# Graph layer with routed experts on one core: token counters as a table, and three small GpSimd jobs of the middle stage handed to a transfer and to ScalarE

## The chip, the cores and the metric

The kernel runs on one core of a Trainium2 chip. A core has a matrix engine (TensorE, PE in the profile, with its weight loads shown apart as PEld), a vector engine (VectorE, DVE), a scalar engine (ScalarE, ACT), a general engine (GpSimd, POOL) and a queue engine (SyncE, SP) that here only issues transfers. Engines run on their own and meet at semaphores: an instruction waits until a counter has reached a value, and a finished instruction raises a counter. The metric is the device time of one execution in microseconds (us). Three runs of the kernel before took 1539.47, 1539.72 and 1540.53 us, so the median is 1539.72 us. A change within 0.2% (3.1 us) is not told from no change.

## The reference, cut to what matters

There are 12,500 tokens of 256 numbers, and an edge list of which only the first 12,500 entries of `src` and `dst` matter here.

```python
xn = layernorm(x)
# graph part: heads 4 x 64; softmax over the heads
xt = (xn @ W).reshape(-1, 4, 64)
alpha = softmax(leaky_relu(alpha_l[src] + alpha_r[dst], 0.01), axis=1)
tmp = einsum('nh,nhd->nd', alpha[:n], xt[dst[:n]])     # a row of a table, gathered by dst
# linear attention with 8 heads, elu + 1, over all tokens
x = x + broadcast(tmp over heads) + mix(xn)
# routed experts: 8 experts, each token goes to the one with the largest logit
logits = layernorm(x) @ gate_w + gate_b
idx, prb = argmax(softmax(logits)), its probability
pos = how many earlier tokens chose the same expert     # kept while pos < capacity
y = (relu(rows @ w1[e] + b1[e]) @ w2[e] + b2[e]) * prb
x = x + nan_to_num(y)
```

## The kernel before, in words

The 12,500 tokens are worked on as 25 tiles of 500 (`NS = 25`, `TS = 500`): 125 partitions (`T`) with 4 tokens each (`J`). There are three stages, each a block in which every engine has an instruction list of its own.

**First stage** (L146 to L625, to 367 us). Layer norm, queries and keys, and per token a row of `graph_table` (values, scores and gate logits of each of 4 heads) and of `alpha_l_table`, both written to memory in HBM. What the gate logits owe to the token itself stays on chip in `xl_all`, and the edge indices are read into `idx_all` (both hold all 25 tiles). GpSimd sets constants here, among them the counters `tokn` and `ntokn` (L325, L327).

**Middle stage** (L628 to L1227, 367 to about 762 us), the one that the change touches. Each engine walks the 25 tiles with `over_steps` (L735): tiles 0 and 1 written out, tiles 2 to 21 in a hardware loop of two tiles per turn, tiles 22 to 24 written out. Buffers with two halves are picked by `par`, the parity of the tile. In step `s`:

- SyncE (`step`, L771) waits until the output of tile `s` is in `xd`, stores it, waits for the matrix products of tile `s` and loads the input of tile `s + 2` into `x_sb`. In step 22 it then starts the loads of the first expert's weights (`first_expert`, L749).
- GpSimd (`step`, L821) waits for the first product `pr` of tile `s` (the gathered rows of the same parity have then been read), issues the eight indirect transfers that gather the rows of tile `s + 2` (`gather`, L792: four into `gl`, four into `gx`, L797), copies the indices of tile `s + 3` out of `idx_all` (`idx_of`, L786, once the gathers that read that half of `idx` have landed), copies the logits of tile `s + 2` into the last columns of `x_sb` (`xl_of`, L801) and steps the two token counters by 500 (`token_of`, L806: `tokn` holds token number plus one, `ntokn` its negative). It does so after ScalarE has used the counters of tile `s - 1` (`s_at_ready`).
- ScalarE (`step`, L905): the square root of the variance (`root`), the transposed inverse (`inverse_t`), a copy of the queries (`q_copy`), two exponentials (`logit_exp`, `att_exp`), and `one_hots` (L869). That last one turns the place given to each token into a row and a column one-hot: `nprb`, eight `Abs` activations into `away`, then, after waits for its own results and for `s_token`, twelve `Relu` activations. In four of these the counters are the bias and the scale (L890). Square root and exponential are in different activation tables, so every step has two table loads.
- VectorE (`step`, L1055): `rows_of` (sum `xd`, statistics), `den_of`, `logits` (its first instruction, L1009, needs the root), `choose`, `att_scores` and `q_scaled` of tile `s + 1`, `place` (writes `prb`, `block_f`, `row_f`), `att_sum` of tile `s + 1` (the three large `pr` instructions).
- TensorE (`step`, L1205): `x_part(s + 1)` (needs `x_sb` with its logits, `s_xl`), `inverse`, `listed(s - 1)` (the one-hots, L1200), `den_spread`, `positions`, `mix(s + 1)` (L1175) and `q_ksum(s + 2)`.

Ahead of its steps GpSimd copies two sets of indices, gathers tiles 0 and 1, copies the indices of tile 2 and then the logits of tiles 0 and 1 (L812 to L819).

**Third stage** (L1229 on, to the end). The eight experts on the rows listed in the middle stage. The change does not touch it.

Of the kernel before, what the change touches and what calls it, by code (L numbers as in the profile page):

```python
# [56 lines left out]
def gps_layer(nc, x, src, dst, gnn_w, attn_l, attn_r, wq, wkv, wproj, bproj,  # L57
# [49 lines left out]
    with base:  # L107
        def sb(name, shape, dt=F32):
            return sb_in(base, name, shape, dt)
# [14 lines left out]
        tokn = sb("tokn", [T, J])  # L124
        ntokn = sb("ntokn", [T, J])
# [20 lines left out]
        with ExitStack() as ph, nc.Block() as block:  # L146
# [134 lines left out]
            def _(pool):  # L281
# [43 lines left out]
                nc.gpsimd.iota(tokn[:, :], [[1, J]], base=1 - TS, channel_multiplier=J,  # L325
                               allow_small_or_imprecise_dtypes=True)
                nc.gpsimd.iota(ntokn[:, :], [[-1, J]], base=TS - 1, channel_multiplier=-J,  # L327
# [300 lines left out]
        with ExitStack() as ph, nc.Block() as block:  # L628
# [61 lines left out]
            s_idx = sem_in(ph, "s_idx")  # L690
# [35 lines left out]
            s_token = sem_in(ph, "s_token")  # L726
# [5 lines left out]
            x_in, gat, x_out = [s_x_in0, s_x_in1], [s_gat0, s_gat1], [s_x_out0, s_x_out1]  # L732
            NATT, NPR, NLG, NROUTE, NPLACE, NAWAY = 7, 3, 3, 11, 4, 9
# [14 lines left out]
            def _(sp):  # L748
# [18 lines left out]

                load(0, 0)
                load(1, 1)

                def step(s, par, h, ahead):  # L771
                    sp.wait_ge(s_x2_ready, 2 * (s + 1))
                    split_dma(sp, tok(out, s, D), xd[:, par, :, :], T, x_out[par])
                    if ahead == 2:
                        sp.wait_ge(s_mix_mm, 2 * (s + 1))
                        load(s + 2, par)
                    if ahead == 2 and isinstance(s, int) and s == NS - 3:
                        first_expert()
# [6 lines left out]
            def _(pool):  # L785
                def idx_of(s, par, n):  # L786

                    pool.wait_ge(gat[par], 32 * J * n)
                    nc.gpsimd.tensor_copy(idx[:, par, :, :], idx_all[:, bass.ds(s, 1), :, :].rearrange("p a n j -> p (a n) j"))\
                      .then_inc(s_idx, 1)  # L790

                def gather(s, par):  # L792
                    pool.wait_ge(s_idx, s + 1)
                    passed(pool, s_pool_passed)
                    for n, (to, of) in enumerate(((gl, table_l), (gx, table))):
                        for j in range(J):
                            pool.indirect_dma_start(out=to[:, par, j, :], out_offset=None, in_=of,  # L797
                                                    in_offset=bass.IndirectOffsetOnAxis(ap=idx[:, par, n, j:j + 1], axis=0))\
                                .then_inc(gat[par], 16)

                def xl_of(s, par):  # L801
                    pool.wait_ge(s_mix_mm, 2 * (s - 1))
                    nc.gpsimd.tensor_copy(x_sb[0:T, par, :, D:MW],
                                          xl_all[:, bass.ds(s, 1), :, :].rearrange("p a j e -> p (a j) e")).then_inc(s_xl, 1)

                def token_of(s):  # L806
                    pool.wait_ge(s_at_ready, 3 * J * s)
                    passed(pool, s_pool_passed)
                    nc.gpsimd.tensor_scalar(tokn[:, :], tokn[:, :], float(TS), None, ALU.add).then_inc(s_token, 1)
                    nc.gpsimd.tensor_scalar(ntokn[:, :], ntokn[:, :], float(TS), None, ALU.subtract).then_inc(s_token, 1)  # L810

                idx_of(0, 0, 0)  # L812
                idx_of(1, 1, 0)
                gather(0, 0)
                gather(1, 1)
                idx_of(2, 0, 1)
# [4 lines left out]
                def step(s, par, h, ahead):  # L821
                    if ahead == 2:
                        pool.wait_ge(s_pr, NPR * s + 1)
                        gather(s + 2, par)
                        if not (isinstance(s, int) and s + 3 >= NS):
                            idx_of(s + 3, 1 - par, h + par + 1)
                        xl_of(s + 2, par)
                    token_of(s)
# [6 lines left out]
            def _(act):  # L835
# [16 lines left out]
                for c in range(KC):  # L852
                    act.wait_ge(s_mixw_mm, KC)
                    act.activation(mix_w[:, c, :], psM[:, KC + c, 0:MW], ACT.Copy).then_inc(s_mixw_set, 1)

# [13 lines left out]
                def one_hots(s):  # L869
# [14 lines left out]
                    act.wait_ge(s_token, 2 * (s + 1))  # L884
                    passed(act, s_act_passed)
                    for j in range(J):
                        act.activation(at_row[:, j, :], away[:, j, 0:T3], ACT.Relu, bias=1.0, scale=-1.0)\
                           .then_inc(s_at_ready, 1)
                        for n, (v, nv) in enumerate(((tokn, ntokn), (prb, nprb))):
                            act.activation(at_block[:, j, n, :], away[:, j, T3:T3 + NB], ACT.Relu, bias=v[:, j:j + 1],  # L890
                                           scale=nv[:, j:j + 1]).then_inc(s_at_ready, 1)
# [13 lines left out]
                def step(s, par, h, ahead):  # L905
# [6 lines left out]
                    if ahead > 0:  # L912
                        att_exp(s + 1)
                        one_hots(s)
                    else:
                        last_rows(s)
# [5 lines left out]
            def _(dve):  # L922
# [160 lines left out]
                dve.wait_ge(s_token, 2 * NS)  # L1083
                dve.wait_ge(s_perm_mm, NS - 1)
                for j in range(J):
                    for n, v in enumerate((tokn, prb)):
                        nc.vector.tensor_scalar(at_block[:, j, n, :], upto[:, T3:T3 + NB], blk[:, j:j + 1], v[:, j:j + 1],
# [627 lines left out]
```

## Time and profile before

| | before |
|---|---|
| median of three runs | 1539.72 us |
| the profiled execution | 1540.95 us |
| its span, first to last instruction | 1539.1 us |
| mean granted TensorE clock, share of full | 0.943 |
| busy PE, DVE, ACT, POOL | 1426.4, 1122.5, 952.0, 727.3 us |
| middle stage, about | 367 to 762 us |

The profile gives each engine's busy time, then the span in 40 slices, then the groups of instructions by cost, and the trace behind it can be asked for one stretch, one line or all waits. "Busy" says how much an engine did, not whether the end depended on it: for that the waits are read. A wait "A <- B" means that A's engine sat idle and that B's end is what let it go on; "issue" stands for time in which nothing that the profile shows was waited for. In rows of a timeline the first number is the start, the second the length, and the bracket at the end is the idle time just before. A line number is that of the kernel before.

### The profile page before, as it was taken

Reading aid. Unit: us, or ns where it says so; the run is one execution under the profiler, and the core shown is the slowest. Engines: PE = TensorE matmul, PEld = TensorE weight load, DVE = VectorE, ACT = ScalarE, POOL = GpSimd, SP = SyncE. Lnnn points to the kernel's source line nnn. Section 1 sums busy time; section 2 is a strip of 40 time slices with the busy share of each in tenths; the row PEclk is TensorE's granted clock in tenths of the full one; section 3 lists DMA queues with packets and bytes.
Section 4 is the critical chain, followed back from the end, with each engine's and each line's share of the span. In section 5 each row is a group of like instructions: output and inputs, shape, how many; then the busy total and the mean of one; then the engine's idle time right before and its main releaser. Section 6 shows DMA issues by size and latency. Waiting matters only on the chain. (4 is left out here: it accounts for less than half of the span.)

```text
span 1539.1 us, 30428 instructions
## 1 busy us (share of the span) xinstructions
PE 1426.4 (93%) x9008; PEld 1282.6 (83%) x9008; DVE 1122.5 (73%) x2832; ACT 952.0 (62%) x2017; POOL 727.3 (47%) x704
## 2 busy tenths in 40 slices
PE   5999999998799898899579999999999999999995
PEld 4999999997677777777469999999999999999994
DVE  5888888883678778778536867767776776877764
ACT  2555555542477777777556767667676676767662
POOL 1100000003788888888243446445446445455533
PEclk8999999997788988988779999999999999999998
DMA  4434333333344444445312121213113131122000
GB/s 85 87 80 80 86 83 74 86 73 74 93 111 109 117 109 111 116 109 157 73 31 78 31 57 44 71 39 97 43 40 91 40 95 43 39 69 53 7 15 19
DMA packets 128116, 112.13 MB, mean 73 GB/s; under 512 B 66078, under 2 KB 113887, under 8 KB 127946
## 3 DMA queue, kind: packets, MB, share of 16 engines
q1 hardware_dynamic: 75206, 72.73, 19.0%
q0 software_dynamic: 52864, 38.82, 11.5%
q8 instruction: 24, 0.39, 0.1%
q14 instruction: 22, 0.18, 0.0%
HBM read 76.17 MB, written 43.85 MB: 78 GB/s over the span
## 5 line engine op out<-in xcount | busy, mean ns | idle before, releaser
L1390 POOL DMA_INDIRECT out<-q_all,to_i x128 | 176.3, 1378 | 328.6 <-issue 293.8
L1592 DVE TENSOR_TENSOR h_lo<-q_all,h_hi 128x496 fp32r<-128x496 f32 x256 | 173.8, 679 | 197.7 <-PE psY L1653 88.4
L1468 ACT ACTIVATE h_hi<-psH,b_sb 128x496 fp32r<-128x496 f32 x256 | 172.6, 674 | 232.7 <-PE psH L1676 225.7
L1653 PE MATMUL psY<-w_hi,h_hi 128*124 128x256 f32 x1024 | 289.2, 282 | 0.0
L1653 PE MATMUL psY<-w_hi,h_lo 128*124 128x256 f32 x1024 | 287.1, 280 | 0.0
L1653 PE MATMUL psY<-w_lo,h_hi 128*124 128x256 f32 x1024 | 286.8, 280 | 0.0
L1653 PEld LDWEIGHTS psY<-w_lo,h_hi 128*124 128x124 f32 x1024 | 188.9, 184 | 8.9
L1653 PEld LDWEIGHTS psY<-w_hi,h_hi 128*124 128x124 f32 x1024 | 188.8, 184 | 8.0
L1377 POOL DMA_INDIRECT q_all<-out,from_i x112 | 164.5, 1469 | 54.8 <-issue 54.8
L1653 PEld LDWEIGHTS psY<-w_hi,h_lo 128*124 128x124 f32 x1024 | 189.1, 185 | 0.0
L1470 ACT ACTIVATE q_all<-psH,b_sb 128x496 f32<-128x496 f32 x256 | 170.8, 667 | 0.0
L1676 PE MATMUL psH<-xt_hi,w_hi 128*128 128x496 f32 x512 | 158.4, 391 | 2.4 <-issue 2.1
L1175 PE MATMUL psM<-mix_w,qp 128*125 128x264 f32 x400 | 135.1, 509 | 25.1 <-DVE qp L952 25.1
L1676 PE MATMUL psH<-xt_hi,w_lo 128*128 128x496 f32 x512 | 157.4, 389 | 0.0
L1676 PE MATMUL psH<-xt_lo,w_hi 128*128 128x496 f32 x512 | 156.6, 387 | 0.0
L292 POOL TENSOR_SCALAR rstd<-mv 125x4 f32<-125x4 f32 x25 | 5.7, 229 | 297.0 <-DVE mv L410 297.0
L1175 PEld LDWEIGHTS psM<-mix_w,qp 128*125 128x125 f32 x400 | 100.5, 257 | 52.2 <-DVE qp L952 27.4
L797 POOL DMA_INDIRECT gl<-alpha_l_table,idx x100 | 123.2, 1232 | 34.1 <-issue 29.2
L797 POOL DMA_INDIRECT gx<-graph_table,idx x100 | 121.7, 1217 | 30.5 <-issue 30.2
L1676 PEld LDWEIGHTS psH<-xt_hi,w_lo 128*128 128x128 f32 x512 | 96.6, 189 | 19.4
L1676 PEld LDWEIGHTS psH<-xt_lo,w_hi 128*128 128x128 f32 x512 | 96.6, 189 | 19.2
L371 ACT ACTIVATE eq<-psR 128x500 f32<-128x500 f32 x50 | 29.5, 589 | 89.7 <-PE psR L585 89.7
(241 smaller groups left out, 3366.6 us busy)
## 6 DMA issues: line engine op xcount, KB each, us to landing
x_sb<-in_x SPq DMA_DIRECT2D x50, 448.0 KB
q_all<-in_L_ffn_w SPq DMA_DIRECT2D x16, 1024.0 KB
graph_table<-tab_sb SPq DMA_DIRECT2D x25, 511.0 KB
out<-xd SPq DMA_DIRECT2D x25, 448.0 KB
x_sb<-in_x SPq DMA_DIRECT2D x50, 52.0 KB
out<-q_all,to_i POOLq DMA_INDIRECT x128, 4.3
q_all<-out,from_i POOLq DMA_INDIRECT x112, 4.5
gl<-alpha_l_table,idx POOLq DMA_INDIRECT x100
```

The costliest lines, as they stand in the source:

```text
L292: nc.gpsimd.tensor_scalar(rstd[:, :], mv[:, :, 1], EPS, None, ALU.add).then_inc(s_var_ready, 1)
L371: act.activation(eq[:, c, :], psR[c][:, 0:TS], ACT.Exp).then_inc(s_eq_exp, 1)
L797: pool.indirect_dma_start(out=to[:, par, j, :], out_offset=None, in_=of, in_offset=bass.IndirectOffsetOnAxis(ap=idx[:, par, n, j:j + 1], a ...
L1175: ins = nc.tensor.matmul(psM[0:T, j, 0:MW], qp[:, kc, j * T:(j + 1) * T], mix_w[:, kc, :], start=False, stop=kc == KC - 1)
L1377: pool.indirect_dma_start(out=xr[:, slot, j, :], out_offset=None, in_=out, in_offset=bass.IndirectOffsetOnAxis(ap=at[:, j:j + 1], axis=0), ...
L1390: pool.indirect_dma_start(out=out, in_=o_sb[:, par, j, :], in_offset=None, out_offset=bass.IndirectOffsetOnAxis(ap=to_i[:, par, j:j + 1], ...
L1468: act.activation(h_hi[:, f % 4, :], psH[f % 2][:, 0:TS3], ACT.Relu, bias=b1_sb[:, bass.ds(e * NF + f, 1)]).then_inc(s_hhi_ready, 1)
L1470: act.activation(hf[:, f % 4, :], psH[f % 2][:, 0:TS3], ACT.Relu, bias=b1_sb[:, bass.ds(e * NF + f, 1)]).then_inc(s_hf_ready, 1)
L1592: nc.vector.tensor_tensor(h_lo[:, f % 4, :], hf[:, f % 4, :], h_hi[:, f % 4, :].bitcast(F32), ALU.subtract).then_inc(s_hlo_ready, 1)
L1653: ins = nc.tensor.matmul(psY[par][j // 2][0:T3, (j % 2) * D:(j % 2 + 1) * D], hh[:, f % 4, j * T3:(j + 1) * T3], w[:, f, :], start=f == 0 ...
L1676: ins = nc.tensor.matmul(psH[f % 2][:, 0:TS3], w[:, kc, f * P:(f + 1) * P], xt[:, par, kc, :], start=n == 0, stop=n == 3 * KC - 1)
```

## The change

The two counters become tables `tok_all` and `ntok_all` with a column for each of the 100 (tile, j) pairs, set once in the first stage; `token_of` and the semaphore `s_token` are gone, and with them the wait in `one_hots` and the one before the last tile's columns. ScalarE reads the tables at an address that depends on the loop counter. `idx_of` moves to SyncE as a transfer from `idx_all` to `idx`, behind the load of tile `s + 2`, with a semaphore for each half. `xl_of` moves to ScalarE between `att_exp(s + 1)` and `one_hots(s)`.

```diff
-                nc.gpsimd.iota(tokn[:, :], [[1, J]], base=1 - TS, channel_multiplier=J,
+                nc.gpsimd.iota(tok_all[:, :], [[TS, NS], [1, J]], base=1, channel_multiplier=J,
                                allow_small_or_imprecise_dtypes=True)
-                nc.gpsimd.iota(ntokn[:, :], [[-1, J]], base=TS - 1, channel_multiplier=-J,
+                nc.gpsimd.iota(ntok_all[:, :], [[-TS, NS], [-1, J]], base=-1, channel_multiplier=-J,
...
             def _(sp):
+                def idx_of(s, par, n):
+                    sp.wait_ge(gat[par], 32 * J * n)
+                    sp.dma_start(idx[:, par, :, :], idx_all[:, bass.ds(s, 1), :, :].rearrange("p a n j -> p (a n) j"))\
+                      .then_inc(idx_in[par], 16)
+
+                for s in range(2):
+                    sp.dma_start(idx[:, s, :, :], idx_all[:, s, :, :]).then_inc(idx_in[s], 16)
                 load(0, 0)
                 load(1, 1)
+                idx_of(2, 0, 1)
...
                         load(s + 2, par)
+                        if not (isinstance(s, int) and s + 3 >= NS):
+                            idx_of(s + 3, 1 - par, h + par + 1)
...
             def _(pool):
-                def idx_of(s, par, n):
-                    pool.wait_ge(gat[par], 32 * J * n)
-                    nc.gpsimd.tensor_copy(idx[:, par, :, :], idx_all[:, bass.ds(s, 1), :, :].rearrange("p a n j -> p (a n) j"))\
-                      .then_inc(s_idx, 1)
-                def gather(s, par):
-                    pool.wait_ge(s_idx, s + 1)
+                def gather(s, par, n):
+                    pool.wait_ge(idx_in[par], 16 * n)
...
-                def xl_of(s, par):
-                    pool.wait_ge(s_mix_mm, 2 * (s - 1))
-                    nc.gpsimd.tensor_copy(x_sb[0:T, par, :, D:MW],
-                                          xl_all[:, bass.ds(s, 1), :, :].rearrange("p a j e -> p (a j) e")).then_inc(s_xl, 1)
-                def token_of(s):
-                    pool.wait_ge(s_at_ready, 3 * J * s)
-                    passed(pool, s_pool_passed)
-                    nc.gpsimd.tensor_scalar(tokn[:, :], tokn[:, :], float(TS), None, ALU.add).then_inc(s_token, 1)
-                    nc.gpsimd.tensor_scalar(ntokn[:, :], ntokn[:, :], float(TS), None, ALU.subtract).then_inc(s_token, 1)
-                idx_of(0, 0, 0)
-                idx_of(1, 1, 0)
-                gather(0, 0)
-                gather(1, 1)
-                idx_of(2, 0, 1)
+                gather(0, 0, 1)
+                gather(1, 1, 1)
...
                     if ahead == 2:
                         pool.wait_ge(s_pr, NPR * s + 1)
-                        gather(s + 2, par)
-                        if not (isinstance(s, int) and s + 3 >= NS):
-                            idx_of(s + 3, 1 - par, h + par + 1)
-                        xl_of(s + 2, par)
-                    token_of(s)
+                        gather(s + 2, par, h + 2)
...
             def _(act):
+                def xl_of(s, par):
+                    act.wait_ge(s_mix_mm, 2 * (s - 1))
+                    act.activation(x_sb[0:T, par, :, D:MW],
+                                   xl_all[:, bass.ds(s, 1), :, :].rearrange("p a j e -> p (a j) e"), ACT.Copy)\
+                       .then_inc(s_xl, 1)
...
                     act.wait_ge(s_away, NAWAY * (s + 1))
-                    act.wait_ge(s_token, 2 * (s + 1))
...
-                        for n, (v, nv) in enumerate(((tokn, ntokn), (prb, nprb))):
-                            act.activation(at_block[:, j, n, :], away[:, j, T3:T3 + NB], ACT.Relu, bias=v[:, j:j + 1],
-                                           scale=nv[:, j:j + 1]).then_inc(s_at_ready, 1)
+                        act.activation(at_block[:, j, 0, :], away[:, j, T3:T3 + NB], ACT.Relu,
+                                       bias=tok_all[:, bass.ds(s * J + j, 1)], scale=ntok_all[:, bass.ds(s * J + j, 1)])\
+                           .then_inc(s_at_ready, 1)
+                        act.activation(at_block[:, j, 1, :], away[:, j, T3:T3 + NB], ACT.Relu, bias=prb[:, j:j + 1],
+                                       scale=nprb[:, j:j + 1]).then_inc(s_at_ready, 1)
...
                     if ahead > 0:
                         att_exp(s + 1)
+                    if ahead > 1:
+                        xl_of(s + 2, par)
+                    if ahead > 0:
                         one_hots(s)
```

## Rows read from the trace of the kernel before

**Rows 1.** Windows: us, busy PE, PEld, DVE, ACT, POOL, then granted clock, DMA share, GB/s.

```profile
400.00:750.00 350.00, 317.78 (x1687) 264.34 (x1686) 275.02 (x1041) 259.79 (x671) 273.48 (x275) 0.87 0.47 118
```

**Rows 2.** Waits, 366 to 760 us: total us, times, longest.

```profile
ACT nprb L875 <- DVE row_f L1052: 59.2, 24, 2.9
DVE rstdb L1009 <- ACT std L863: 29.2, 23, 1.8
DVE xd L993 <- PE psM L1175: 25.4, 17, 10.6
ACT at_row L887 <- POOL ntokn L810: 16.9, 22, 0.9
DVE att L957 <- DMA gx<-graph_table,idx: 1.7, 1, 1.7
```

**Rows 3.** Timeline of one loop step, 540 to 555 us.

```profile
540.08 0.92 POOL L789 COPY idx<-idx_all 125x8 int32 x1
...
542.45 0.31 ACT L887 ACTIVATE at_row<-away 125x124 f32<-125x124 f32 x1 [0.83 <-POOL ntokn L810]
...
546.44 1.28 ACT L863 ACT_TABLE_LOAD   x1
...
548.06 0.18 DVE L1009 RECIPROCAL rstdb<-std 125x4 f32<-125x4 f32 x1 [1.67 <-ACT std L863]
...
553.54 0.21 ACT L875 ACTIVATE nprb<-prb 125x4 f32<-125x4 f32 x1 [2.44 <-DVE row_f L1052]
...
554.46 0.92 POOL L789 COPY idx<-idx_all 125x8 int32 x1
```

**Rows 4.** The page's groups: count, busy, mean ns, idle before.

```profile
L797 POOL DMA_INDIRECT gx<-graph_table,idx x100 | 121.7, 1217 | 30.5 <-issue 30.2
```

**Rows 5.** Timeline of step 0, before the waits for the counters begin.

```profile
409.26 0.21 ACT L875 ACTIVATE nprb<-prb 125x4 f32<-125x4 f32 x1 [1.65 <-DVE row_f L1052]
...
415.92 1.28 ACT L863 ACT_TABLE_LOAD   x1
...
417.54 0.18 DVE L1009 RECIPROCAL rstdb<-std 125x4 f32<-125x4 f32 x1 [0.82 <-issue]
```

**Rows 6.** Timeline: a long mix and a short one, and the roots behind.

```profile
552.31 6.64 PE L1175 MATMUL psM<-mix_w,qp 128*125 128x264 f32 x16 [1.33 <-DVE qp L952]
...
562.45 0.18 DVE L1009 RECIPROCAL rstdb<-std 125x4 f32<-125x4 f32 x1 [0.32 <-ACT std L863]
...
567.18 3.83 PE L1175 MATMUL psM<-mix_w,qp 128*125 128x264 f32 x16 [0.47 <-DVE qp L952]
...
577.35 0.18 DVE L1009 RECIPROCAL rstdb<-std 125x4 f32<-125x4 f32 x1 [1.83 <-ACT std L863]
...
736.34 0.18 DVE L1009 RECIPROCAL rstdb<-std 125x4 f32<-125x4 f32 x1 [0.32 <-ACT std L863]
```

**Rows 7.** Timeline of the start of the middle stage, GpSimd, SyncE and TensorE.

```profile
367.08 0.64 SPq L42 DMA_DIRECT2D x_sb<-in_x  x1
...
368.45 1.48 POOL L797 DMA_INDIRECT gl<-alpha_l_table,idx  x1 [1.01 <-issue]
...
386.89 1.85 POOL L797 DMA_INDIRECT gx<-graph_table,idx  x1 [0.30 <-issue]
...
393.42 0.35 POOL L819 COPY x_sb<-xl_all 125x32 f32<-125x32 f32 x2
...
393.73 3.85 PE L1168 MATMUL psM<-x_sb,ident_x 126*125 126x264 f32 x8 [7.32 <-issue]
```

**Rows 8.** DMA issues: size, then median us from issue to landing.

```profile
q_all<-in_L_mix_Wq SPq DMA_DIRECT2D x1, 256.0 KB, 4.1
```

**Rows 9.** Loop operands on ScalarE's queue (L847): min, median, max ns.

```profile
L847 ACTq FUSED_REGOPS  x20: 51/51/57, 430.9 to 706.9; - x20
```

**Rows 10.** SyncE's last load of a step, and a DMA window behind it.

```profile
546.14 0.88 SPq L43 DMA_DIRECT2D x_sb<-in_x  x1
...
549.00:551.00 2.00, 1.98 (x21) 1.80 (x19) 1.62 (x12) 1.73 (x4) 1.70 (x2) 1.00 0.42 72
```

More of the change, by code:

```diff
@@ L123, in gps_layer @@
         desc = sb("desc", [T, J, E])
-        tokn = sb("tokn", [T, J])
-        ntokn = sb("ntokn", [T, J])
+        tok_all = sb("tok_all", [T, NS * J])
+        ntok_all = sb("ntok_all", [T, NS * J])
         upto = sb("upto", [T, T3 + NB])
@@ L689, in gps_layer @@
             s_x_in1 = sem_in(ph, "s_x_in1")
-            s_idx = sem_in(ph, "s_idx")
+            s_idx0 = sem_in(ph, "s_idx0")
+            s_idx1 = sem_in(ph, "s_idx1")
             s_gat0 = sem_in(ph, "s_gat0")
@@ L725, in gps_layer @@
             s_pos_mm = sem_in(ph, "s_pos_mm")
-            s_token = sem_in(ph, "s_token")
             s_place = sem_in(ph, "s_place")
@@ L732, in gps_layer @@
             x_in, gat, x_out = [s_x_in0, s_x_in1], [s_gat0, s_gat1], [s_x_out0, s_x_out1]
+            idx_in = [s_idx0, s_idx1]
             NATT, NPR, NLG, NROUTE, NPLACE, NAWAY = 7, 3, 3, 11, 4, 9
@@ L1082, in _ @@
                 dve.wait_ge(s_place, NPLACE * NS)
-                dve.wait_ge(s_token, 2 * NS)
                 dve.wait_ge(s_perm_mm, NS - 1)
                 for j in range(J):
-                    for n, v in enumerate((tokn, prb)):
-                        nc.vector.tensor_scalar(at_block[:, j, n, :], upto[:, T3:T3 + NB], blk[:, j:j + 1], v[:, j:j + 1],
+                    for n, v in enumerate((tok_all[:, (NS - 1) * J + j:(NS - 1) * J + j + 1], prb[:, j:j + 1])):
+                        nc.vector.tensor_scalar(at_block[:, j, n, :], upto[:, T3:T3 + NB], blk[:, j:j + 1], v,
                                                 ALU.is_equal, ALU.mult).then_inc(s_at_ready, 1)
```

## The prediction, as it was put on record

> **What bounds the kernel now.** I read three views: windows of the middle stage, its waits, and a timeline of single steps. In the windows no engine of the middle stage is full: PE 317.8, DVE 275.0, ACT 259.8, POOL 273.5 of 350 us, and TensorE's granted clock is 0.87 [rows 1]. POOL's busy time hides that it is nonetheless the pace: its transfers of 1.217 us follow each other with 0.305 us of issue between (30.5 us over 100) [rows 4], so eight gathers are 8 x 1.52 = 12.2 us, and from one copy of indices to the next it is 554.46 - 540.08 = 14.38 us [rows 3]. The rest, 2.2 us, is the two copies and the two counter steps. The list of waits has none of GpSimd among the large ones; others wait for it: ScalarE 22 times, 16.9 us, before `at_row` (L887), each time for `ntokn` [rows 2].
>
> What follows a late L887 is a ring between ScalarE and VectorE. L887 late, so the table load for the root late, so the root late, and VectorE has already been standing 1.67 us at L1009 for it [rows 3]; in all 23 such waits, 29.2 us [rows 2]. From L1009 VectorE works to `row_f`, which starts ScalarE's next `nprb`. So the wait for the counters is on the path, and in most steps nothing else would catch it.
>
> **The ring without the wait, from rows.** L1009 to `nprb`: 553.54 - 548.06 = 5.48 us [rows 3]. `nprb` to the table load, in a step in which the counters were ready: 415.92 - 409.26 = 6.66 us [rows 5]. Table load to L1009: 548.06 - 546.44 = 1.62 us [rows 3], and 417.54 - 415.92 = 1.62 us in step 0 too [rows 5]. Sum 13.76 us against GpSimd's 14.38: 0.62 us less a step. The mean wait is 16.9/22 = 0.77; the other 0.15 is ScalarE's own turn-round at that point and stays.
>
> **The change part by part.**
>
> *The wait for the counters goes.* 22 steps x 0.62 = 13.6 us off ScalarE's part. What is late next is VectorE's own work: its wait at L1009 shrinks from 1.67 to 1.05 us, so in an ordinary step the whole 0.62 passes. It doesn't where the matrix product was long. With a `mix` of 6.64 us VectorE stood only 0.32 us at L1009 [rows 6], so there only some 0.3 passes. I counted six such waits of 0.32 to 0.34 us (first 446.44, last 736.34 [rows 6]). 16 x 0.62 + 6 x 0.3 = 11.7 us.
>
> *TensorE's clock.* A `mix` takes 3.83 us at 2.4 GHz and 6.64 us when it falls nearly whole into a stretch at 1.2 GHz [rows 6]; before each of them TensorE had been idle for `qp` or on very small products. A long one costs its own step and the one behind it: that next step was 577.35 - 562.45 = 14.90 us [rows 6], 0.52 above 14.38. Steps of another length move where the slow stretches fall. With none of the long ones up to 6 x (0.32 + 0.5) = 4.9 us more come off, with as many as now nothing. I can't work out the pattern; that it repeats now every four steps says only that this step length locks to it. I take two of six avoided: 1.6 us.
>
> *The start is on the path, and gets longer.* TensorE sits 7.32 us until GpSimd has copied the logits of tile 0 at 393.42, behind 16 gathers that began at 368.45 [rows 7]. They now can't begin until a transfer of indices has landed, which SyncE issues at 367.08, where now its first load is [rows 7]. Lower bound: 0.64 us of issue [rows 7] and nothing else, 367.7, where the old gather began at 368.45: 0, or 0.1 less for the copy of tile 2's indices that is gone. Upper: 4.1 us, which 256 KB took to land [rows 8], and then the 1.01 us that the first gather stood [rows 7]: 372.2, 3.7 us late. The transfer is 4 KB in 125 pieces; I take a landing after 3 us and 0.3 of issue, 370.4: 1.9 us, less the copy's 0.1 = +1.8 us. The Trainium skill ("DMA: Bandwidth & Descriptors", section "Anatomy of one DMA") gives a fixed cost of about 2.0 us to a transfer of any size; by that the start would be some 0.8 us later and the sum 1 us lower. No row here shows a small transfer by itself.
>
> *Indices in the loop.* SyncE issues them behind the load that starts at 546.14 and takes 0.88 to issue [rows 10], at about 547.0; the wait for the older gathers ahead of it is long over, since they were all issued by 540.08. Only the next step's stores queue behind it, some 12 us later. GpSimd wants them at the end of the next `pr`, over 7.5 us later (that product is running when GpSimd stands at its copy at 554.46 [rows 3]). The DMA share is down to 0.42 by 549 to 551 [rows 10]. Cost 0; with the 4.1 us of [rows 8] still 0. If it did land late, gathers have most of a step in hand: of all steps one waited for them, 1.7 us [rows 2].
>
> *GpSimd.* 12.2 us of work in 13.76. A gather beside VectorE's large products was once stretched from 1.2 to 1.85 us [rows 7]; two of them a step give 13.5, still under 13.76. The Trainium skill ("SBUF — State Buffer", section "SBUF: two separate sides") makes the port pair that VectorE and GpSimd share an exclusive lock for the length of an instruction. The 0.92 us copy, which did 8 numbers a partition beside a running `pr`, agrees with it; the rule speaks against this change in that the gathers now start just where the second and third `pr` instructions run, but even a stretch in every step leaves the sum as it is.
>
> *ScalarE's new copy.* 32 numbers a partition, about as `lex` or `nprb`, 0.2 us, in the 2.44 us in which ScalarE waits for `row_f` [rows 3]. Cost 0. Without that cover it would be 0.2 x 23 = 5 us.
>
> *Addresses from the loop counter.* Eight operands a step in 20 loop steps; one such computation is 0.051 us on ScalarE's queue [rows 9]. Bounds: 0 if the queue does them while the engine works, 8 x 0.051 x 20 = 8.2 us if each stands on the path. The activations are 0.3 to 0.5 us each and nothing waits between the twelve, so I take 0. The wider constants in the first stage fall where GpSimd is idle: 0.
>
> *Tail.* The one wait for gathers (1.7 us) is in step 23, under the expert loads. The gathers start a little earlier, the steps are shorter: 0, give or take 1. The third stage is not touched: 0.
>
> **Sum.** -11.7 - 1.6 + 1.8 = -11.5 us on the profiled execution's 1540.95 (span 1539.1 and 1.85 around it): 1529.4. The median of the runs is 1.2 us below that execution, so 1528.2.
>
> **Rivals.**
>
> 1. *The slow clock takes over (slower).* If every `mix` fell into a slow stretch, a step would be L1009 to `mix` 567.18 - 562.45 = 4.73, `mix` 6.64, and from its end (558.95) to an L1009 no longer held by the table load, 562.45 - 0.3, 3.2 us: 14.57 us. Now the mean over 22 steps is (736.34 - 417.54)/22 = 14.49. That gives 22 x 0.08 = +1.8, with the start +3.6: 1543.3. It decides from about 18 of 22 long ones: the 16.1 us of 22 x (14.49 - 13.76), less the start's 1.8, over 0.8 each. For it: shorter steps come at the clock in another phase, and one in four is long now. Against: a long one lengthens the step and so moves out of its phase.
> 2. *Addresses on the path.* 8.2 us of the gain gone: 1536.4, just inside faster. For it: the sequencer may not run ahead past the wait on `away`. Against: only the first of the twelve stands right behind a wait.
> 3. *The gap is not the counters'.* If L887 waits for ScalarE's own `away`, the profile has named the wrong one, nothing is saved and the start remains: 1541.5. Against: step 0, with the same instructions and the counters ready, took the 6.66 [rows 5].
> 4. *Indices late.* If the small transfers sit behind the loads for more than the 7.5 us and then most of a step, gathers hold `att_scores`: from there each us late costs up to 23; one us gives 1551. Against: the DMA row above.
>
> **Chances.** Forecast 0.80, rival 1 0.05, rival 2 0.09, rival 3 0.03, rival 4 0.03. About 0.2% (3.1 us) is what a measurement here tells from no change. Faster takes the forecast and most of rival 2: 0.87; same 0.06; slower 0.07 (rivals 1 and 4, part of 3). Range: at the low end no long `mix` and an instant start, 1539.7 - 13.6 - 3 = 1523, less 1 of the tail, 1522; at the high end rival 2 nearly whole, 1536.
>
> **What would show it.** Right: no wait L887 <- POOL; steps of about 13.8 us from L1009 to L1009; L1009 waiting about 1 us; GpSimd waiting for `pr` in each step; the first gather near 370.4 and the first xl copy near 395.2; the third stage as long as before. Wrong: gaps between the twelve activations (rival 2), `mix` of 6.64 us in most steps (1), GpSimd waiting for a transfer or `att` waiting for `gx` (4).

## The result and the profile after

The changed kernel takes 1527.08 us (median of 4 runs, 1525.46 to 1527.51), the kernel before 1540.12 us beside it (1539.47 to 1540.58). The ratio is 0.9914, 95% interval 0.9897 to 0.9931. The forecast was 1528.2.

(In one series, of two kernels below, the times were longer, the kernel before at 1582.88 us as well; those two kernels were run once more, beside a kernel before at 1540.18.)

The profiled execution took 1525.46 us, its span is 1523.6. I cut both spans at the same instructions: the first memset of the middle block on VectorE, and the reciprocal `rstdb` (L1009 before, L1007 after) of each step.

| stretch | before | after | difference |
|---|---|---|---|
| first stage, to the block's first memset | 367.2 | 365.1 | -2.1 |
| memset to `rstdb` of step 0 | 37.1 | 39.0 | +1.9 |
| step 0 to 1 | 13.2 | 13.2 | -0.1 |
| steps 1 to 23, 22 steps | 318.8 | 304.1 | -14.7 |
| step 23 to 24 | 15.0 | 15.7 | +0.7 |
| all behind it | 787.8 | 786.6 | -1.2 |

The first and the last line belong to code that the change doesn't touch. The first stage ended between 365.0 and 366.4 us in the experiments of the normal series, whichever kernel ran, so about 2 us of the profiled difference are its variation. The medians differ by 13.0 and the spans by 15.5: the profiled execution before was 0.8 us above its median, the one after 1.6 below.

The window of the middle stage after; columns as in [rows 1]:

```profile
400.00:750.00 350.00, 322.52 (x1708) 267.87 (x1706) 281.01 (x1078) 269.45 (x712) 225.77 (x182) 0.87 0.47 119
```

GpSimd is busy 47.7 us less than in [rows 1], though the stretch holds slightly more of the stage (1708 matmuls to 1687). ScalarE is busy 9.7 us more. The clock and the DMA share are the same.

The waits from 366 to 760 us after, to be laid beside [rows 2] (total us, times, longest):

```profile
ACT nprb L869 <- DVE row_f L1050: 55.3, 24, 2.8
...
POOL gl L803 <- DVE pr L980: 36.7, 20, 3.3
...
DVE rstdb L1007 <- ACT std L857: 18.0, 22, 1.1
```

The wait of `at_row` for `ntokn` is gone, and `rstdb` waits 18.0 us where it waited 29.2. GpSimd now has a large wait of its own: it stands for `pr` in nearly each step.

One loop step after, timeline from 540 to 555 us, beside [rows 3]:

```profile
540.94 0.77 SPq L772 DMA_DIRECT2D idx<-idx_all  x1
541.01 0.18 DVE L1007 RECIPROCAL rstdb<-std 125x4 f32<-125x4 f32 x1 [0.93 <-ACT std L857]
...
544.03 0.22 ACT L846 ACTIVATE x_sb<-xl_all 125x32 f32 x1
...
546.50 0.21 ACT L869 ACTIVATE nprb<-prb 125x4 f32<-125x4 f32 x1 [2.26 <-DVE row_f L1050]
...
549.16 0.31 ACT L880 ACTIVATE at_row<-away 125x124 f32<-125x124 f32 x1
549.26 1.40 POOL L803 DMA_INDIRECT gl<-alpha_l_table,idx  x1 [1.76 <-DVE pr L980]
...
553.15 1.28 ACT L857 ACT_TABLE_LOAD   x1
...
554.77 0.18 DVE L1007 RECIPROCAL rstdb<-std 125x4 f32<-125x4 f32 x1 [0.94 <-ACT std L857]
```

This is the ring (the chain of waits that closes on itself once a step), as forecast: L1007 to `nprb` 546.50 - 541.01 = 5.49, `nprb` to table load 553.15 - 546.50 = 6.65, table load to L1007 1.62; together 13.76. `at_row` follows its `away` without a gap.

The start, timeline, beside [rows 7]:

```profile
364.94 1.57 SPq L776 DMA_DIRECT2D idx<-idx_all  x2
...
365.06 0.17 DVE L921 MEMSET heads<- 128x128 f32 x1 [3.26 <-PEq L146]
...
368.03 1.49 POOL L803 DMA_INDIRECT gl<-alpha_l_table,idx  x1 [29.20 <-issue]
...
392.24 0.37 POOL L811 COPY x_sb<-xl_all 125x32 f32<-125x32 f32 x2
...
392.57 3.85 PE L1165 MATMUL psM<-x_sb,ident_x 126*125 126x264 f32 x8 [8.30 <-issue]
```

The first gather starts 368.03 - 365.06 = 2.97 us behind the memset, before it was 368.45 - 367.2 = 1.25: 1.7 us later. The copies of logits are only 1.0 us later (392.24 - 365.06 = 27.18, before 393.42 - 367.2 = 26.22), because a gather that took 1.85 us before [rows 7] took 1.21 here. The other 0.9 us are the first `mix`: 4.72 us at a granted clock of 0.79, where it took 3.85 at 0.97.

### The profile page after: what moved, and what is told of

Its sections match the earlier page's. It is cut to its first block and busy times, and to the rows that moved or that the text cites. A ratio compares the mean times of both kernels' runs of the same rounds, so it can differ in the third digit from the quotient of the medians.

```text
span 1523.6 us, 30383 instructions
## 1 busy us (share of the span) xinstructions
PE 1424.1 (93%) x9008; PEld 1281.1 (84%) x9008; DVE 1120.9 (74%) x2832; ACT 954.2 (63%) x2040; POOL 675.9 (44%) x606
## 5 line engine op out<-in xcount | busy, mean ns | idle before, releaser
L1172 PE MATMUL psM<-mix_w,qp 128*125 128x264 f32 x400 | 136.4, 514 | 15.5 <-DVE qp L950 15.5
L371 ACT ACTIVATE eq<-psR 128x500 f32<-128x500 f32 x50 | 29.4, 588 | 88.7 <-PE psR L585 88.7
```

What stands on the lines that cost most here:

```text
L371: act.activation(eq[:, c, :], psR[c][:, 0:TS], ACT.Exp).then_inc(s_eq_exp, 1)
L1172: ins = nc.tensor.matmul(psM[0:T, j, 0:MW], qp[:, kc, j * T:(j + 1) * T], mix_w[:, kc, :], start=False, stop=kc == KC - 1)
```

## The experiments

Each run was made beside the kernel before, and its ratio is to that. "Steps" are `rstdb` to `rstdb` in the profiled execution.

**1. The table alone.** The kernel before, with only the counters replaced by the table:

```diff
-                    token_of(s)
...
-                    act.wait_ge(s_token, 2 * (s + 1))
...
-                            act.activation(at_block[:, j, n, :], ..., bias=v[:, j:j + 1], scale=nv[:, j:j + 1])
+                        act.activation(at_block[:, j, 0, :], ..., bias=tok_all[:, bass.ds(s * J + j, 1)],
+                                       scale=ntok_all[:, bass.ds(s * J + j, 1)])
```

> The kernel before with the table of counters alone: the copies of indices and logits stay on GpSimd. Theory (the ring): GpSimd's cycle falls from 14.38 by the two counter steps (0.73 + 0.51) to 13.1 us, under the 13.76 us of the ring ScalarE-VectorE, so the ring sets the step as in the kernel after, and the start isn't longer. 22 steps from 14.49 to about 13.8: 1525.5 us, 1 to 2 us under the kernel after. Rival (the copies too must go, since the large products hold them up to 1.4 us on the shared port): GpSimd stays the pace near 14 us, time 1530 us or more.

Measured: 1528.22 us (1526.54 to 1529.27), ratio 0.9925 [0.9909, 0.9942]. The 22 steps took 304.4 us, against 304.1 with the whole change. `rstdb` waits as briefly as there:

```profile
DVE rstdb L1002 <- ACT std L855: 16.8, 20, 1.1
```

The table by itself gives the whole gain of a step. It missed its 1525.5 by 2.7 us. Of these, 1.0 is the start: the first gather stood at the old 1.25 us behind the memset, but the first `mix` took 4.86 us at a granted clock of 0.76, and the first `rstdb` came 38.14 us behind the memset, before it was 37.1. Another 1.0 is the last step (16.00 us, before 14.98). The rest isn't placed.

**2. The two moves alone.** The changed kernel, with the counters kept on GpSimd:

```diff
                         gather(s + 2, par, h + 2)
+                    token_of(s)
...
                     act.wait_ge(s_away, NAWAY * (s + 1))
+                    act.wait_ge(s_token, 2 * (s + 1))
```

> The kernel after with the counters stepped on GpSimd as before, behind the gathers, and ScalarE waiting for them; the two copies are moved. Theory (amount and order both): GpSimd's cycle is 12.2 + 1.24 = 13.4 us, under 13.76, but the gathers wait for pr, start about 1 us late and end while the next pr holds the port, so the counters come 0.5 to 1.2 us after its end where ScalarE wants them 0.9 us after it: a wait of 0 to 0.4 us a step, 1527 to 1536 us, middle 1531. Rival (amount alone counts): no wait at L887's place, 1527 us. Rival (the counters' own time counts in full): as before, 1540 us.

Measured: 1531.0 us (1529.83 to 1531.92), the middle of what was expected, ratio 0.9939 [0.9922, 0.9955]; steps mostly 13.80 to 13.83, the 22 of them 307.6 us.

```profile
ACT at_row L889 <- POOL ntokn L812: 5.5, 20, 1.0
```

The wait for the counters shrinks to 0.28 us a step. So each half alone gives most of the gain: the halves overlap and don't add.

**3. The start.** The changed kernel, with the indices of the first two tiles copied by GpSimd again, and without SyncE's two transfers for them:

```diff
+                for s in range(2):
+                    nc.gpsimd.tensor_copy(idx[:, s, :, :], idx_all[:, s, :, :]).then_inc(idx_in[s], 16)
                 gather(0, 0, 1)
```

> The kernel after with the first two sets of indices copied by GpSimd as before, the rest by transfer. Theory: the first gather starts 1.4 us behind the block's start instead of 3.1, and everything behind it up to 1.7 us earlier: 1525.5 us against 1527.1, a ratio to before some 0.001 lower than the kernel after has. Rival (the start is hidden or given back by the clock): 1527 us, no difference.

Measured: 1524.11 us (1524.0 to 1527.14), ratio 0.9903 [0.9886, 0.992], which by itself is not told from the changed kernel's 0.9914. Memset to first `rstdb` is 36.7 us, 2.25 less than with the change. The profile:

```profile
364.97 0.32 POOL L806 COPY idx<-idx_all 125x8 int32<-125x8 int32 x2 [26.26 <-POOLq L146]
...
366.30 1.49 POOL L801 DMA_INDIRECT gl<-alpha_l_table,idx  x1 [1.01 <-issue]
```

The first gather is 1.7 us earlier than in the changed kernel. The first `mix` starts 1.25 us earlier and takes 3.73 us at a granted clock of 1.00 instead of 4.72: together the 2.25. So the transfer does hold up the start, as predicted. But the clock takes some of it back: the second `mix` is a long one here (6.86 us), and the first two steps are 13.84 and 14.32 us where they were 13.17 and 13.63.

**4. More work on GpSimd before.** If GpSimd's throughput sets the step, half a microsecond more for it must lengthen each step by that much:

```diff
                         xl_of(s + 2, par)
+                        pool.wait_ge(s_pad, s)
...
+                        nc.gpsimd.memset(pad[:, 0:512], 1.0).then_inc(s_pad, 1)
                     token_of(s)
```

> The kernel before with one more fill of 125x512 on GpSimd in each step, ahead of the counter steps (about 0.5 us). Theory (GpSimd's throughput is the pace of the kernel before): the step goes from 14.49 to about 15.0, 22 to 23 steps of 0.5: +12 us, 1551 us, with GpSimd still never waiting for pr. Rival (only the place of the counters behind the gathers counts, GpSimd has slack): +0 to +3 us.

Measured: 1539.56 us (10 runs), ratio 0.9999 [0.9989, 1.0008]. A clear miss. One step's timeline, GpSimd and the products beside it:

```profile
582.50 1.42 DVE L983 TENSOR_TENSOR pr<-gx,att 125x1152 f32<-125x1152 f32 x1
582.64 1.32 POOL L791 COPY idx<-idx_all 125x8 int32 x1
...
583.95 0.78 DVE L987 TENSOR_TENSOR pr<-pr 125x576 f32<-125x576 f32 x1
584.06 0.51 POOL L832 MEMSET pad<- 125x512 f32 x1
584.56 0.26 POOL L811 TENSOR_SCALAR tokn<-tokn 125x4 f32<-125x4 f32 x1
584.76 0.46 DVE L989 TENSOR_TENSOR pr<-pr 125x288 f32<-125x288 f32 x1
584.80 0.50 POOL L812 TENSOR_SCALAR ntokn<-ntokn 125x4 f32<-125x4 f32 x1
...
585.41 0.31 ACT L892 ACTIVATE at_row<-away 125x124 f32<-125x124 f32 x1 [0.79 <-POOL ntokn L812]
```

And the same place in the kernel before, timeline, GpSimd and VectorE:

```profile
541.13 0.72 POOL L809 TENSOR_SCALAR tokn<-tokn 125x4 f32<-125x4 f32 x1
541.81 0.46 DVE L984 TENSOR_TENSOR pr<-pr 125x288 f32<-125x288 f32 x1
541.84 0.51 POOL L810 TENSOR_SCALAR ntokn<-ntokn 125x4 f32<-125x4 f32 x1
```

The fill took its 0.51 us, and `tokn` shrank from 0.72 to 0.26. The copy of indices (8 numbers a partition) reads as 1.32 us here and 0.92 in [rows 3]: it ends when the first `pr` ends, whenever it began. In both kernels `ntokn` ends when the third `pr` ends. Of the 2.2 us that the profile counts as GpSimd's work behind the gathers, the larger part is standing beside VectorE's products.

**5. The same counters at another place.** The kernel before, with the counters between the `gl` and the `gx` gathers; GpSimd issues exactly what it issued:

```diff
                     for n, (to, of) in enumerate(((gl, table_l), (gx, table))):
+                        if tok and n == 1:
+                            token_of(s - 2)
                         for j in range(J):
...
-                    token_of(s)
+                    if ahead != 2:
+                        token_of(s)
```

> The kernel before with one change of order: the two counter updates of a step stand between its four gl gathers and its four gx gathers, not behind the index copy. GpSimd issues exactly the same instructions. Theory 1 (GpSimd's own throughput paces the step, as the prediction had it): the same work, so steps stay at 14.38 us and the time at 1540 (1539 to 1541). Theory 2 (the ring is: end of the products on VectorE, then index copy, logits copy and counters on GpSimd, then ScalarE's one-hots; GpSimd's gathers are done 0.9 us before the products are): the counters leave the ring, ScalarE no longer waits for GpSimd, steps fall to 13.75 to 13.85 as with the table alone, and the time to 1528 (1526 to 1531). In between, if the index copy now ends later than the products: steps of 14.0, 1532.

In this series the ratio was 0.9729 [0.971, 0.9747] (1541.12 us beside 1582.88); most steps were 13.9 to 14.05, six of them 15.9 to 17.1. Beside a kernel before that was 43 us longer than in the other series it shows the sign, not the size, so it was run again:

> The same kernel as the one with the counters between the gl and the gx gathers, once more, because in its first run the kernel before stood at 1583 us instead of 1540 (granted clock 0.926 instead of 0.94 over the span), so that the ratio measured the chip as well. That run showed steps of 14.0 us with some of 15.9 to 17.1. Theory 2 (the ring from the products over the copies and counters to the one-hots): with the kernel before at 1540, 1528 to 1532, most steps 13.8 to 14.0. Theory 1 (GpSimd's throughput): 1540.

Measured: 1532.28 us (1530.7 to 1534.21), at the upper edge of what theory 2 gave, ratio 0.9951 [0.9934, 0.9967]; 18 steps of 13.98 to 14.09. GpSimd's own timeline of one of them:

```profile
543.32 1.21 POOL L799 DMA_INDIRECT gl<-alpha_l_table,idx  x1 [0.30 <-issue]
544.57 0.25 POOL L811 TENSOR_SCALAR tokn<-tokn 125x4 f32<-125x4 f32 x1
544.77 0.23 POOL L812 TENSOR_SCALAR ntokn<-ntokn 125x4 f32<-125x4 f32 x1
...
551.02 0.59 POOL L789 COPY idx<-idx_all 125x8 int32 x1
...
552.59 1.39 POOL L799 DMA_INDIRECT gl<-alpha_l_table,idx  x1 [0.82 <-DVE pr L985]
```

Away from the products the counters take 0.25 and 0.23 us, not 0.72 and 0.51. With the same instructions GpSimd now waits 0.82 us for `pr`, and the step is 0.4 us shorter. Together with experiment 4 that refutes the throughput and shows the ring. 0.24 us of the step were lost elsewhere: VectorE's rounding in `place()` took 0.41 us instead of 0.17, ending as a gather's issue ended:

```profile
548.29 1.21 POOL L799 DMA_INDIRECT gx<-graph_table,idx  x1 [0.30 <-issue]
...
549.06 0.41 DVE L1053 TENSOR_SCALAR block_f<-block_f 125x4 f32<-125x4 f32 x1
```

**6. A fill behind the gathers, changed kernel.** For this one nobody waits:

```diff
                         gather(s + 2, par, h + 2)
+                        pool.wait_ge(s_pad, s)
...
+                        nc.gpsimd.memset(pad[:, 0:1200], 1.0).then_inc(s_pad, 1)
```

> The kernel after with one more fill of 125x1200 on GpSimd in each step behind the gathers (about 1.1 us), that nobody waits for. Theory: GpSimd's cycle is 12.2 + 1.1 = 13.3 us, under the ring's 13.74, so nothing moves: 1527 us, and GpSimd's wait for pr (1.76 us a step) shrinks by the fill. Rival (GpSimd is still near the bound because gathers and products block each other): +0.3 us a step, 1534 us.

Measured: 1535.27 us, ratio 0.9953 [0.993, 0.9975], in two groups: 3 of 10 runs at 1524.5 to 1526.2, slightly under the forecast 1527, 7 at 1534.7 to 1538.4. The median is the number of the rival, but not by its 0.3 us in every step. The profile is of the second group. Most of its steps are 13.74, and four are 15.98 to 16.43:

```profile
644.07 1.21 POOL L805 DMA_INDIRECT gx<-graph_table,idx  x1 [0.30 <-issue]
...
644.87 1.56 DVE L1050 TENSOR_SCALAR block_f<-slotf 125x4 f32<-125x4 f32 x1
...
645.28 1.11 POOL L821 MEMSET pad<- 125x1200 f32 x1
...
660.81 2.05 DVE L1053 TENSOR_SCALAR block_f<-block_f 125x4 f32<-125x4 f32 x1
661.71 1.12 POOL L821 MEMSET pad<- 125x1200 f32 x1
```

Instructions of 0.17 to 0.20 us on 4 numbers took 1.56 and 2.05, until the gather and then the fill were over (645.28 + 1.11 = 646.39, 661.71 + 1.12 = 662.83). They are in the ring, and make 1.4 and 1.9 of the 2.2 and 2.5 us by which these two steps are longer than 13.74; VectorE also waits for `psB` in them (0.84 and 0.21 us in the first), which it doesn't in an ordinary step. So GpSimd had time for a microsecond more, and yet could stop VectorE, if its work fell on `place()`. Why only some of the runs fall into this isn't shown.

**7. More work in the ring.** Two `Abs` more on ScalarE, before the others of `away`, on the changed kernel:

```diff
                     passed(act, s_act_passed)
+                    for k in range(2):
+                        act.activation(pad[:, k, :], upto[:, 0:T3], ACT.Abs, bias=row[:, k:k + 1], scale=-1.0)\
+                           .then_inc(s_away, 1)
                     for j in range(J):
```

> The kernel after with two more Abs activations of 125x124 on ScalarE in each step, between nprb and away (0.58 us by the pitch of 0.29). Theory (ScalarE's one-hots are in the ring): every one of 23 steps grows by 0.58 us, 13.74 to 14.3: +13 us, 1540 us. Rival (another ring of the same length, VectorE and TensorE, sets 13.74 and ScalarE has slack): less than half of it, 1530 us or less.

Measured: 1540.15 us, ratio 1.0004 [0.9995, 1.0014]; the 22 steps are 13.2 us longer, 0.60 each on the mean. That the mean comes out at the 0.58 put in is partly luck: ordinary steps take 14.17 and 14.30 us in turn, 0.50 more than 13.74, and the rest comes from five steps of 15.05 to 15.26, each behind a `mix` of some 6.7 us. Still most of what is added counts: the ring of ScalarE and VectorE binds the changed kernel.

**8. Two row one-hots to GpSimd.** On top of experiment 3:

```diff
-                    for j in range(J):
+                    for j in range(2):
                         act.activation(away[:, j, 0:T3], ...)
...
+                        for j in (2, 3):
+                            nc.gpsimd.tensor_scalar(at_row[:, j, :], upto[:, 0:T3], row[:, j:j + 1], None, ALU.is_equal)
```

> As e3_start, and the row one-hots of two of the four j are written by GpSimd with one comparison each, behind its gathers, in the 1.7 us in which it waits for pr; ScalarE does four activations less (two of 0.29, two of 0.19 us of pitch). Theory (the ring is ScalarE's): ScalarE's part falls by 0.97 us, VectorE has 0.76 to 0.9 us of wait to give, so the step falls by about 0.76 to 13.0 us: 22 x 0.76 = 17 us under e3_start, 1509 us; up to 0.4 us a step lost where GpSimd and the large products block each other: 1517. Rival (TensorE's long products or its order bind at 13.7): 1523 to 1526 us.

Measured: 1525.16 us (1521.03 to 1528.76), ratio 0.99 [0.9873, 0.9926], where the rival had it. A miss: a microsecond left ScalarE's ring and steps only fell to 13.66 to 13.70. The waits:

```profile
DVE qp L959 <- PE psB L1161: 24.0, 44, 4.4
...
DVE rstdb L1016 <- ACT std L865: 1.3, 5, 0.4
```

`rstdb` hardly waits any more. VectorE waits for the product `psB` instead, 44 times: that speaks for a second ring through TensorE (`mix`, `xd`, the inverse, the lists, the spread), which would be 0.06 us behind the first. But GpSimd, which now has the one-hots beside the products, no longer waits for `pr` either: eight gathers and the two one-hots fill its 13.68 us. And the first rounding in `place()` takes 0.43 to 0.58 us in several of these steps instead of 0.17. Which of the three holds the step, this run doesn't tell.

**9. The expert loads a little later.** On top of experiment 3, SyncE waits for the last tile's gathers before it starts the expert weights:

```diff
                     if ahead == 2 and isinstance(s, int) and s == NS - 3:
+                        sp.wait_ge(gat[0], 32 * J * (NS // 2 + 1))
                         first_expert()
```

> As e3_start, with the loads of the first expert's weights issued only once the gathers of tile 24 have landed (a wait on SyncE ahead of first_expert). Theory: the last step's wait for gx (2.8 us in e3_start, 2.3 in the kernel after, 1.7 before) is DMA traffic of those loads; it goes, the step 23 to 24 falls from 16.1 to 13.5 or 14: 2.3 us under e3_start, 1521.8 us, and the weights still land before the third stage. Rival (the loads become late for the third stage): gain there lost again, 1524 us or more.

Measured: 1521.44 us (1520.42 to 1522.46), ratio 0.988 [0.9863, 0.9896]. Step 23 to 24 takes 13.18 us where it took 15.71 in the changed kernel; the wait of `att` for `gx` (2.31 us) is gone, and what lies behind that step is as long as before (787.0 us, 786.6 in the changed kernel). This version beats both kernels.

**10. One row one-hot to VectorE.** On top of experiment 9, outside the ring, behind `place()`:

```diff
                     if ahead > 0:
+                        nc.vector.tensor_scalar(at_row[:, 3, :], upto[:, 0:T3], row[:, 3:4], None, ALU.is_equal)\
+                          .then_inc(s_at_ready, 1)
                         att_sum(s + 1, 1 - par)
```

> The version with the two first copies back on GpSimd and the deferred expert loads, and one of the four row one-hots made by VectorE in one comparison behind place(): takes 0.31 us of Abs and about 0.2 to 0.3 us of Relu out of ScalarE's one-hots (0.485 by pitches), adds 0.34 us to VectorE outside the ring. Theory 1 (only ScalarE's ring binds): steps fall from 13.74 to 13.26, 22 steps give -10.6, 1511. Theory 2 (a second ring, TensorE's products at the low granted clock with the inverse, the token lists and the spread in between, binds at 13.68): steps 13.65 to 13.7, 1520 (1518.5 to 1521.5), VectorE's wait for std gone and a wait for psB or psM in its place. Were the clock high, the second ring would be shorter and steps nearer 13.3.

In the series with the longer times: 1589.5 us beside 1582.88, ratio 1.0047 [1.0031, 1.0063], steps mostly of 16 to 18 us; VectorE waited 42.9 us in all before `qp`, put down to no engine by the profile, and 29.4 for `psB`. The cause of that I leave open. The second run:

> The same kernel as the one with one row one-hot on VectorE, once more for the same reason: there it took 1589.5 beside 1583 for the kernel before, with steps of some 16 us in which VectorE waited 2 to 3 us for the spread product psB. With the kernel before at 1540, theory 2 (second ring through TensorE) has 1520 (1518.5 to 1521.5), theory 1 (only ScalarE's ring) 1511. A third possibility, after that run: the shorter ring asks more of TensorE in each us, the clock is granted less often, and the time is no better than 1525 on any chip.

Measured: 1521.11 us (1520.11 to 1522.31), ratio 0.9875 [0.9859, 0.9892]: not to be told from experiment 9. But it is not the forecast steps. From 529 us on they alternate between 13.36 and 13.84, and TensorE's granted clock is 1.00 (2.4 GHz) in 500 to 700 us, where it was 0.88 in the changed kernel. The first of the long ones, at 542.29, holds this:

```profile
546.11 0.68 DVE L952 TENSOR_TENSOR qp<-psB,q_all 128x500 f32<-128x500 f32 x1 [0.21 <-PE psB L1158]
...
547.54 0.49 DVE L1050 TENSOR_SCALAR block_f<-block_f 125x4 f32<-125x4 f32 x1
```

0.32 us are again the rounding, held until a gather's issue ended (546.85 + 1.21 = 548.06), and 0.21 is the wait for the spread product `psB`. That product is not where the clock was low: it takes 2.04 us in the changed kernel too, at a granted clock of 1.00 (555.95 to 558.00 us), and what is granted 0.69 to 0.71 there is `mix`. Theory 2 had the size right and, for the later steps, the reason wrong: no low clock is needed. Since GpSimd waits for `pr` here (1.43 and 1.78 us around this step), its throughput is not what holds the step. The third possibility is refuted: the clock was granted more, not less.

## Why the prediction was right, and where not

*The wait for the counters goes: right.* -0.62 us a step was forecast from 13.76 against 14.38; the steps are 13.72 to 13.76, and experiment 1 shows that this is the table's doing alone. What was late next is what was named: VectorE stands 0.93 us at L1007 (1.05 forecast), and experiment 7 shows that most of what is added to the ring through ScalarE comes out in the step (0.50 of 0.58 us).

*"GpSimd is the pace": wrong.* The step that fails is the sentence that has 12.2 us of gathers and 2.2 us of copies and counters make up 14.38. The gathers are that long. The 2.2 us are mostly standing: the copy of indices reads 0.92 us in [rows 3], 0.59 where it began later beside the same product (experiment 5), and 0.16 each at the start (0.32 for two, experiment 3); the counters read 0.72 and 0.51, away from the products 0.25 and 0.23. Experiments 4 and 5 decide it: half a microsecond more on GpSimd costs nothing, the same work at another place shortens the step. The ring of the kernel before ran through the products: `pr` ends, then the counters can run, `at_row`, the one-hots, the root, VectorE to the next `pr`. The price came out right nonetheless, since 14.38 was read from the trace and 13.76 was built from ScalarE's and VectorE's rows without that sentence. It would have misled for experiment 2: with only the copies gone, GpSimd's 12.2 + 1.24 = 13.4 us are under the ring's 13.76, so by that sentence the whole gain was due; the 22 steps gave 11.2 of the 14.7 us.

The Trainium skill ("SBUF — State Buffer", section "SBUF: two separate sides") has VectorE and GpSimd share a port pair under an exclusive lock, which a VectorE instruction takes in a two-port mode, or with two inputs in SBUF against a GpSimd instruction that reads SBUF. The traces agree: a copy of 8 numbers took 1.32 us beside `pr`, which has two inputs, while the fill of experiment 4, which reads nothing, ran its 0.51 us beside the second `pr`; and a VectorE instruction of 0.17 us took 2.05 beside a gather and a fill. The prediction weighed the rule for the gathers and saw it in the copy of indices, but still counted that copy's 0.92 us as work; the rule would have explained the counters too.

*TensorE's clock: the sign right, the size low.* Two of six long `mix` avoided was my guess; one is left (600.28 us, 6.85 us long, steps of 14.25 and 14.72), so more went. -13.3 was forecast for the 22 steps (-11.7 - 1.6), -14.7 measured. Of the 1.4 between them 0.4 is not the clock: ordinary steps fell by 0.64, not 0.62. The pattern changed as a whole: of the short `mix` of 3.83 us only one is left (615.35 us), and most now take 5.3 to 5.5. Rival 1 did not come about.

*The start: the first gather right, the total partly luck.* +1.8 forecast, +1.9 measured to the first `rstdb`. The first gather is 1.7 us later, and experiment 3 confirms that the transfer is why. But only 1.0 of it reaches the copies of logits, which came at 392.24, 3 us sooner than forecast: the first stage ended 2.1 us sooner, and one gather less was stretched (-0.6). What brings the total back to 1.9 is the first `mix` at a lower granted clock (+0.9), which the prediction had at nothing. The 2.0 us that the Trainium skill gives to a transfer of any size ("DMA: Bandwidth & Descriptors", section "Anatomy of one DMA", written there for transfers that GpSimd issues) stand beside 368.03 - 364.94 = 3.09 us here from the start of SyncE's issue to the first gather, of which some 0.8 is the issue (1.57 for two). My 3.3 was nearer than the 2.0 with an issue of 0.3; how much of the 3.09 is the landing no row tells apart.

*Indices in the loop, ScalarE's copy: right, 0.* GpSimd waits for `pr`, never for a transfer; the copy (0.22 us at 544.03) lies in ScalarE's wait of 2.26.

*Addresses from the loop counter: right, 0.* In step 1, where they are constants, `nprb` to the table load is 6.65 us (422.55 to 429.20), and in the loop step above 6.65 too. Rival 2 is refuted. So is rival 3: `at_row` no longer waits.

*Tail: 0.7 to the bad side.* Inside the 1 us allowed. The last gathers still run under the expert loads: `att` waited 2.31 us where it was 1.7 [rows 2], 2.7 in experiment 1, 5.5 in experiment 8, and 0 with the loads held back.

*The sum.* -11.5 us was forecast, and the medians differ by 13.0 (1540.12 to 1527.08). The spans differ by 15.5, of which 3.3 lie in the stages that the change leaves alone; the 12.2 that are left are the forecast, with 1.4 more from the 22 steps (about 1.0 of it the clock) and 0.7 less from the tail.

## What to carry to other kernels

Before a busy time of GpSimd is taken for work, look for the same operation at a place where VectorE runs nothing large: if it is several times shorter there, the rest is standing, and moving the operation can pay most of what removing it does (0.4 of 0.6 us a step here). The test of a "pace" is to give the engine more to do: at a pace the step grows, with slack it doesn't, and the same test on ScalarE told which ring binds. Compare ordinary steps in it, not the mean alone. A value that depends only on the step's number should be a table, because what is slow about a counter is not its arithmetic but whom it must wait for.

## What the runs showed of the hardware

- A GpSimd instruction for which nobody waits can stop VectorE: two small `TENSOR_SCALAR` of `place()`, 0.17 to 0.20 us by themselves, took 0.41 and 0.49 us beside a gather's issue and 1.56 and 2.05 us beside a gather and a fill. The reductions and the `SCALAR_TENSOR_TENSOR` just around the two longest kept their 0.16 to 0.18 us.
- The gathers had little to lose: beside the second and third `pr` the first of a step took 1.34 to 1.40 us instead of 1.21.
- The spread product (16 small matmuls, 32 rows) does depend on the granted clock: 3.77 us at 0.50 in the start of the stage, 2.04 at 1.00 in the steps. `mix` takes 3.83 us at 1.00, 5.5 at 0.69 and 6.85 at 0.55. From the changed kernel, a timeline and three windows (columns as in [rows 1]):

```profile
377.04 3.77 PE L1152 MATMUL psB<-inv_t,spread_at 32*128 32x125 f32 x16
...
377.04:380.81 3.77, 3.77 (x18) 3.55 (x17) 0.68 (x1) 0.14 (x1) 2.86 (x4) 0.50 0.33 87
555.95:558.00 2.05, 2.05 (x19) 1.97 (x19) 1.71 (x9) 1.74 (x4) 1.75 (x2) 1.00 0.63 127
600.28:607.13 6.85, 6.85 (x19) 5.35 (x19) 4.65 (x15) 5.56 (x19) 4.47 (x4) 0.55 0.24 64
```
- With ScalarE's ring 0.5 us shorter, TensorE was granted 1.00 in 500 to 700 us, and the step gained no more than 0.15 us on the mean, 13.60 against 13.74: in the long ones of its steps the time went into the wait for `psB` and into the rounding held by a gather's issue.
